# Spaced row scatters, quartered weight loads, later row norms and a written-out loop in an attention and expert kernel

## The reference, cut to what matters

```python
h = _layernorm(x) * (1 + ca) + sa
Q, K, V = heads(h, Wq), heads(h, Wk), heads(h, Wv)
scores = Q @ K.T / scale + lambda_attn * (tanh(Q) @ J_attn) @ tanh(K).T
scores = where(causal, -inf, scores)
x = x + ga * (softmax(scores) @ V @ Wo.T + bo)
h = _layernorm(x) * (1 + cb) + sb
expert = argmax(h @ centroids.T)              # one expert of 8 per token
alpha = sigmoid(h . centroids[expert])
y = h + relu(norm(h)*g[expert]+b[expert] @ W1[expert].T + b1[expert]) @ W2[expert].T + b2[expert]
x = x + gb * (alpha * y + (1 - alpha) * h)
```

## Time and profile before

| | |
|---|---|
| median of 3 runs | 809.66 us (809.44 to 812.22) |
| profiled execution | 811.99 us, of which its span is 810.2 us |
| instructions in the span | 17292 |
| mean granted clock of TensorE | 0.939 of full speed |
| TensorE matmuls, busy | 693.0 us (86%) |
| VectorE, busy | 545.7 us (67%) |
| ScalarE, busy | 503.0 us (62%) |
| GpSimd, busy | 259.3 us (32%) |
| DMA, mean | 114 GB/s |

### The profile page before, as it was taken

The page is one execution under the profiler, slowest core; times in us unless marked ns, Lnnn a source line. Parts: engine busy times, 40 slices in busy tenths (PEclk is TensorE's granted clock), DMA queues, the critical chain, the costliest instruction groups (busy, mean ns, idle before and its releaser), DMA issues.

```text
span 810.2 us, 17292 instructions
## 1 busy us (share of the span) xinstructions
PE 693.0 (86%) x5199; PEld 344.7 (43%) x5199; DVE 545.7 (67%) x1249; ACT 503.0 (62%) x1182; POOL 259.3 (32%) x342
## 2 busy tenths in 40 slices
PE   4467999999999999978999998799798889897594
PEld 2252434334334434423344343244343225886594
DVE  6959667787856777745568767478587611798352
ACT  1440677676688767745877676466576578657372
POOL 2028129000214724330156253200344100456543
PEclk9866799999999999978999999799899799999898
DMA  8995914193260708260516093526123353533510
GB/s 226 320 177 216 157 32 133 55 186 76 51 118 2 234 4 157 44 189 29 94 26 210 3 157 60 173 52 121 33 100 100 111 181 96 162 94 118 178 57 10
DMA packets 54723, 92.04 MB, mean 114 GB/s; under 512 B 10161, under 2 KB 26061, under 8 KB 54120
## 3 DMA queue, kind: packets, MB, share of 16 engines
q1 hardware_dynamic: 48444, 79.72, 39.4%
q0 software_dynamic: 3520, 8.42, 3.1%
q10 hardware_dynamic: 2668, 2.78, 1.2%
HBM read 51.04 MB, written 37.90 MB: 110 GB/s over the span
## 4 chain that ended last, share of the span: by engine, by line
PE 55%; DVE 18%; issue 10%; ACT 8%; DMA 4%; another core or an unknown queue 2%; POOL 1%; DVEq 1%; ACTq 1%; SPq 0%; POOLq 0%
PE PS L1248 14%; PE PS L1208 13%; PE PS L1274 13%; ACT arenaA L1030 5%; DVE PS L1694 4%; PE PS L1325 3%; PE PS L1336 3%; DVE block_max L1701 3%; PE PS L1278 2%; DVE arenaA L1371 2%; DVE arenaB L1371 2%; ACT arenaB L948 2%; PE PS L1213 2%; DMA arenaB<-r_den 1%
## 5 line engine op out<-in xcount | busy, mean ns | idle before, releaser
L1030 ACT ACTIVATE arenaA<-PS 128x512 f32<-128x512 f32 (+3 forms) x768 | 333.1, 495 | 188.3 <-PE PS L1278 127.3
L1694 DVE CUSTOM_DVE_ANT_0 PS<-PS,mask 128x1024 f32<-128x1024 f32 (+3 forms) x256 | 261.7, 1035 | 119.0 <-PE PS L1208 104.8
L1274 PE MATMUL PS<-arenaA 99*128 99x512 bf16 (+3 forms) x768 | 228.9, 342 | 30.7 <-ACT arenaA L1030 18.7
L1208 PE MATMUL PS<-arenaA 96*128 96x512 bf16 (+3 forms) x768 | 207.5, 347 | 30.3 <-DVE block_max L1701 10.0
L1274 PEld LDWEIGHTS PS<-arenaA 99*128 99x128 bf16 x768 | 73.2, 99 | 223.7 <-ACT arenaA L1030 143.7
L1248 PE MATMUL PS<-arenaA,Vs 128*9 128x512 f32 (+3 forms) x1536 | 161.1, 496 | 0.0
L1701 DVE TENSOR_REDUCE block_max<-PS 128x8 f32<-128x1024 f32 (+1 forms) x96 | 100.4, 1046 | 37.6 <-PE PS L1213 30.5
L1208 PEld LDWEIGHTS PS<-arenaA 96*128 96x128 bf16 x768 | 68.6, 102 | 99.9 <-DVE maxima L1694 30.5
L1278 PE MATMUL PS<-after,identb 128*128 128x128 bf16 x512 | 105.7, 224 | 0.0
L842 POOL DMA_INDIRECT out_dram<-arenaA x46 | 46.7, 1016 | 103.2 <-DVE arenaA L1371 94.8
L1079 ACT ACTIVATE arenaA<-PS,b1p 128x128 f32<-128x128 f32 x184 | 52.7, 373 | 34.5 <-PE PS L1325 20.1
(11 more groups left out here) (219 smaller groups left out, 687.8 us busy)
## 6 DMA issues: line engine op xcount, KB each, us to landing
arenaA<-k_parts SPq DMA_DIRECT2D x96, 128.0 KB, 8.2
arenaA<-by_expert SPq DMA_DIRECT2D x46, 192.5 KB, 3.7
o_raw<-OT SPq DMA_DIRECT2D x32, 256.0 KB, 3.3
k_parts<-arenaB SPq DMA_DIRECT2D x24, 256.0 KB, 3.8
arenaA<-q_parts SPq DMA_DIRECT2D x16, 384.0 KB, 4.9
q_parts<-arenaB SPq DMA_DIRECT2D x18, 256.0 KB, 3.7
arenaA<-in_L_ffn_W_dram SPq DMA_DIRECT2D x2, 2048.0 KB, 13.2
arenaA<-q_parts SPq DMA_DIRECT2D x16, 256.0 KB, 5.7
```

Of the source, the lines that this page charges most:

```text
L1030: a.activation(PT[:, u % EB, h, off:HALF], PS[:, 4 + n % SB_, off:HALF], ACT.Exp).then_inc(exp_ok, 1)
L1208: last = mm(PS[:, place + c0 // HALF, at:at + c1 - c0], SQ(g, h)[0:KROWS, t * P:(t + 1) * P], SK(g, h)[0:KROWS, c0:c1], start=(at == 0), s ...
L1274: last = mm(bank[:, off:HALF], SK(g, h)[0:MROWS, kb * P:(kb + 1) * P], SQ(g, h)[0:MROWS, qc * HALF + off:(qc + 1) * HALF], start=True, sto ...
L1694: v.tensor_tensor_reduce(out=src, in0=src, in1=mask[:, S - n:S], scale=1.0, scalar=-3e38, op0=ALU.add, op1=ALU.max, accum_out=maxima[:, pl ...
```

## The change

Four things are changed. (1) `scatter_rows` gets the number of a group, and block t of the eight waits until 2 + t units of products of that group are done. The group is the fourth of the body in which the rows are made (middle bodies), and the third of the last body. (2) The turned weights come back in four DMAs of 512 KB in place of one of 2 MB, the k-th of them k units of products later. (3) In the last body the norms of x move from units 0 and 1 of group 1 to units 2 and 3, and all items of `POST_LAST` in group 1 (H0, H1, statistics of h, S, the choice of the expert) one step later. (4) The loops over the middle bodies are Python loops, so that the code of each body stands in the program; the waits compare with constants, and the `sem_inc`s on the `..._turn` semaphores behind them are gone.

```diff
+        W_PARTS = 4
...
-        NORMS_AT = dict(middle=dict(x=(2, 0), h=(3, 0)), last=dict(x=(1, 0), h=(2, 0)))
+        NORMS_AT = dict(middle=dict(x=(2, 0), h=(3, 0)), last=dict(x=(1, 2), h=(2, 0)))
...
-                     1: POST_AT[2], 2: POST_AT[3] + ((9, "D", "pads"),), 3: ((0, "D", "table"),)}
+                     1: tuple((at + 1, kind, k) for at, kind, k in POST_AT[2]), 2: POST_AT[3] + ((9, "D", "pads"),), 3: ((0, "D", "table"),)}
...
                     if body == "last" and g < 2:
-
-                        sp.wait_ge(pv_ok, (b * NG + g + 1) * NU + EB)
-                        sp.dma_start((W1T, W2T)[g], w_turned[:, g * E * FF:(g + 1) * E * FF]).then_inc(w_back, 16)
+                        for k in range(W_PARTS):
+
+                            sp.wait_ge(pv_ok, (b * NG + g + 1) * NU + EB + k)
+                            part = slice(k * E * FF // W_PARTS, (k + 1) * E * FF // W_PARTS)
+                            sp.dma_start((W1T, W2T)[g][:, part], w_turned[:, g * E * FF:(g + 1) * E * FF][:, part]).then_inc(w_back, 16)
...
-            with sp.Fori(1, B - 1) as b:
+            for b in range(1, B - 1):
                 attention(b, "middle")
...
-            def scatter_rows(b):
+            def scatter_rows(b, group):
 
                 pool.wait_ge(pool_step, b * 4 + 4)
-                pool.sem_inc(pool_turn, 1)
                 pool.wait_ge(slots_ok, b + 1)
-                pool.sem_inc(pool_turn, 1)
                 pool.wait_ge(pay_ok, b + 1)
                 pool.sem_inc(rows_made, 1)
                 for t in range(TB):
+
+                    pool.wait_ge(pv_ok, group * NU + EB + 2 + t)
                     g.indirect_dma_start(by_expert, bass.IndirectOffsetOnAxis(ap=slot[:, t:t + 1], axis=0), PAY[:, t, :], None)\
                         .then_inc(sorted_out, 16)
...
-            with pool.Fori(2, B) as b:
+            for b in range(2, B):
                 split_batch(b)
-                send_rows(b - 2)
-            send_rows(B - 2)
+                send_rows(b - 2, (b - 1) * NG + 3)
+            send_rows(B - 2, (B - 1) * NG + 2)
...
-                act.wait_ge(w_back, 32)
+                act.wait_ge(w_back, 2 * W_PARTS * 16)
...
-            with pe.Fori(1, B - 1) as b:
+            for b in range(1, B - 1):
                 attention(b, "middle")
```

More of the change, by code:

```diff
@@ L445, in prepared @@
                 sp.wait_ge(va_ok, b + 1)
-                sp.sem_inc(sp_turn, 1)
             for n in (1, 2):
@@ L484, in load_numerators @@
             def load_numerators(b):
-                if isinstance(b, int):
+                if b >= B - 2:
                     sp.wait_ge(stored, B)
@@ L791, in send_rows @@
                 row_factors(b)
-                scatter_rows(b)
+                scatter_rows(b, group)
                 pool.wait_ge(sorted_out, (b + 1) * TB * 16)
@@ L874, in tanh_q @@
                 act.wait_ge(q32_ok, b + 1)
-                if not (isinstance(b, int) and b == 0):
+                if b > 0:
                     act.wait_ge(stored, b)
@@ L880, in first_q @@
             def first_q(b):
-                if not isinstance(b, int):
+                if b > 1:
                     act.wait_ge(sent, b - 1)
@@ L908, in norm_rows @@
                     act.wait_ge(stored, b)
-                    act.wait_ge(lnt_ok, 1 if isinstance(b, int) else 2)
-                    if not isinstance(b, int):
+                    act.wait_ge(lnt_ok, min(b, 2))
+                    if b > 1:
                         act.wait_ge(rows_made, b - 1)
-                        act.sem_inc(act_turn, 1)
                 row = lambda k: lnt[:, k, bass.ds(b * TB + t, 1)]
@@ L1067, in _ @@
             attention(0, "first")
-            with act.Fori(1, B - 1) as b:
+            for b in range(1, B - 1):
                 attention(b, "middle")
@@ L1139, in project @@
                 else:
-                    start = isinstance(b, int) and b == 0
+                    start = b == 0
                     if start and step == "K0":
@@ L1458, in projected @@
                 part = slice(half * HALF, (half + 1) * HALF)
-                later = not isinstance(b, int) or b > 0
+                later = b > 0
                 if what == "X":
@@ L1490, in after_routing @@
                 dve.wait_ge(route_chain, b * ROUTE_LINKS + n)
-                if not isinstance(b, int):
-                    dve.sem_inc(dve_turn, 1)
             L2 = lambda k: ln2[:, k, :]
@@ L1502, in half_stats @@
                 if half:
-                    last.then_inc(post_chain if isinstance(b, int) and b == B - 1 else done, 1)
+                    last.then_inc(post_chain if b == B - 1 else done, 1)
             def half_norm(b, dst, src, half):
@@ L1674, in maximum @@
                 if kind == "T":
-                    if not (isinstance(group, int) and group == 0):
+                    if group > 0:
                         dve.wait_ge(m_in, group * 16)
@@ L1781, in _ @@
             attention(0, "first")
-            with dve.Fori(1, B - 1) as b:
+            for b in range(1, B - 1):
                 attention(b, "middle")
```

25 lines of the change are left out of this document (4 added, 21 removed).

## The result

The changed kernel takes 774.36 us (median of 6 runs, 772.42 to 775.99), the kernel before in the same comparison 809.55 us: a ratio of 0.9554 [0.9528, 0.9579]. The profiled execution takes 773.26 us, its span is 771.5 us, and the two spans differ by 38.7 us. The kernel before was timed again beside each later set of runs, and its median there went up to 811.75 us; a difference between medians of two sets is good to about 2 us.

A forecast was written before the change was run, and what follows sets the result against it. TensorE bounds most of the span; gains lie in gaps at row-block bursts, the loop's jump and the norms. 811.99 - 14.5 - 5.2 - 5.3 - 1.4 = 785.6 us profiled; median 809.66 - 26.4 = 783.3 us, range 775 to 795.

The forecast's parts named there:

- Spacing: Groups with row blocks: one block per unit of products wins back 5.9 + 5.6 + 3.0 = 14.5 us of 19.0 excess.
- yardstick of 17.57 us: First body's group 3, no burst, unit 1's products to transposed maxima; the burst groups' excess over it: 7.4, 7.1, 4.5 us.
- residue of 1.5 us: Loss left in each burst's place after spacing, chosen between 0 and 8 x 2.49 us.
- Rival (a): Groups with bursts: all 19.0 us come back, 30.9 us in all, 778.8 us; chance 0.15.
- (b): Groups with bursts: stops belong to the traffic as a whole, spacing gives nothing; only 11.9 us, 797.8 us; chance 0.12.
- (e): Each of 24 spaced blocks stops the fetch by itself, 2.49 us a time; slower, 838.6 us; chance 0.03.
- Quarters: Turned weights in four pieces on SyncE: their waits cost nothing, and they get no term of their own.
- Norms: Last body, norms two units later: ScalarE no longer waits 4.01 us for moments; the whole 5.2 us excess counted.
- rival (c): Last body: the norms' move gives nothing, TensorE being held at the turn of those rows; 788.5 us; chance 0.10.
- Loop: Middle bodies written out: the jump goes, 5.3 us, and register work ahead of waits, 1.4 us.
- register work: Middle bodies, ahead of waits: 0.7 us a body, 1.4 in all; may be zero, 3 at most.
- Rival (d): Loop's end costs the same written out, pages of code coming late for another reason; 788.6 us; chance 0.05.

The follow-up runs named there:

- d1: Changed kernel with GpSimd's wait for units of products taken out, so the eight row blocks start back to back once the slots are known: 799.44 us, 0.9862.
- b5: Changed kernel with batch 3's batch statistics moved from group 3 of the first body to a late unit of its group 2: 773.41 us, 0.9553.
- a4: Kernel before with the spacing, the quarters and the norms' place, the two middle bodies still one loop with registers: 782.05 us, 0.9639.
- f1: Changed kernel, eight blocks back to back once slots are known, SyncE's ten transfers beside them in the middle bodies held back five units: 797.33 us, 0.9844.
- b1: Changed kernel with the eight row blocks back to back, but not before the ninth unit of products after the stacks: 796.29 us, 0.9816.
- f2: Changed kernel plus five back-to-back indirect blocks of 16 rows, 4 columns each, into an unread tensor; real blocks spaced, two units later: 792.16 us, 0.9772.
- d2: Changed kernel plus five back-to-back indirect blocks of 128 rows, 385 columns, into an unread tensor; real blocks spaced, two units later: 783.25 us, 0.9651.
- d4: Changed kernel plus five full blocks sent as plain transfers from GpSimd's queue to consecutive rows; real blocks spaced, two units later: 777.65 us, 0.9588.
- d3: Changed kernel plus five back-to-back indirect blocks of 128 rows, 4 of 385 columns, into an unread tensor; real blocks spaced, two units later: 783.06 us, 0.9646.
- e4: Changed kernel plus five back-to-back indirect blocks of 64 rows, 4 columns each, into an unread tensor; real blocks spaced, two units later: 786.69 us, 0.9711.
- b2: Changed kernel with two row blocks back to back for every two units of products: 775.71 us, 0.9577.
- e2: Changed kernel with the row blocks sent in two bursts of four, at units 2 and 6 of the group: 777.79 us, 0.9609.
- a2: Changed kernel with each group's turned weights read back in one transfer, as before the change: 774.40 us, 0.9547.
- a3: Changed kernel with the last body's row norms of x back at their old place, operations behind them not shifted: 777.83 us, 0.9585.

## Why the forecast was 9 us short, step by step

**Spacing: forecast 14.5 us, measured 25.1 by medians and 22.4 by the stretches (d1).** This step failed, by size and not by direction. The yardstick of 17.57 us held 1.8 us of statistics that the other groups lack (b5), 5.4 us in three bursts; and the residue of 1.5 us that I left in each burst's place, 4.5 us, did not appear: R1 is 15.83 where an empty group is 15.77. With both put right the term would have been 24.4; 2.0 of that belong to the loop, which makes R1, R2 and R3 longer by 0.49, 0.48 and 1.08 us with spaced blocks (a4), and 22.4 is what d1's three groups lose. Rival (a) erred by the yardstick too. Rivals (b) and (e) fell: the stop is gone with full traffic in place (in the changed kernel the DMA share of 346 to 354 is 1.03 to 1.10, and TensorE is busy throughout), and 24 single blocks stop nothing.

I had also read the chain of waits short: behind the 2.49 us of the earlier trace rows it stands a second time for the same burst, and the two make 6.9 us. The 2.49 went into the upper bound and into rival (e).

```profile
350.89 4.38 another core or an unknown queue
```

**What the stop is.** I took it for instructions that arrive late. That is not borne out: in the kernel before, no packet of the two instruction queues moves between 506 and 518, while the stop goes from 507.68 to 513.78 and ends. Only these two queues have packets in that window, and neither is an instruction queue (packets, MB, share of 16 engines):

```profile
q1 hardware_dynamic: 1034, 1.68, 52.6%
q0 software_dynamic: 512, 1.58, 38.9%
```

What the runs show is that ScalarE and VectorE get what TensorE has for them late while GpSimd issues indirect blocks one right behind the other. The semaphore events of the traces show it directly. In the changed kernel all 192 units of products raise `pv_ok` within 0.05 us of their recorded end. In the kernel before five do not, all beside a burst: the products that end at 507.23 raise it at 512.28, 5.05 us late, and the others are 0.98 to 3.21 us late. In d1 and f1 the latest is 5.6 us late, in b1 6.5, in f2 3.9, in d2 1.45; in d4 none beside the plain transfers is over 0.06. (The ends of matmuls are modelled, so the end of the work and the signal can't be told apart.) Bytes do not matter (d3), nor SyncE's transfers (f1), and fewer rows do not lessen it (e4, f2); plain transfers do not do it (d4), and pairs and fours cost little (b2, e2). Through what TensorE's signals are held, and why fewer rows make it worse, stays open; that the shorter distance of 1.15 us does it was not tested by itself.

**Quarters: forecast nothing, measured nothing (a2).**

**Norms: forecast 5.2 us, in place 6.4, but only 3.5 by themselves (a3).** ScalarE's 4.01 us wait was rightly read and is gone, and TensorE is not held at the turn of those rows: it turns them at 561.77 and idles 0.45 us behind, so rival (c) fell. Unforeseen was that writing out the loop takes 1.7 us from GpSimd's chain to the moments in the last body as well.

**Loop: forecast 5.3 + 1.4 us, measured 7.7 (a4).** The jump is 4.0 to 4.8 us and not 5.3, since I compared it with a first body whose stretch is not the same. The register work, 1.4 forecast, is 1.5 in the groups of the middle bodies and 0.55 at the entry; R3 and the stretch ahead of it, in the last body, are 1.1 and 0.3 us longer too; I had priced nothing there, since no register is read, and did not test whether the counts behind the waits make it. Rival (d) fell.

By medians the parts are 25.1 + 0.0 + 3.5 + 7.7 = 36.3 us, against 35.2 for all together; by ratios to the kernel before they are 24.9 - 0.6 + 2.5 + 6.9 = 33.7 against 36.1. Of the 8.8 us that the forecast lacked, the spacing alone has 10.6 by medians and 7.9 by the stretches; the norms' 1.7 us too much and the loop's 1.0 too little nearly cancel.

## What to carry to other kernels

Five or more indirect DMAs of GpSimd sent back to back held up the other engines here, for nearly as long as the row of them lasted and however small they were. Let each wait for a unit of TensorE's work, which costs nothing where nobody waits for the last. A stretch without the disputed thing is a yardstick only if it holds the same other work: list what stands in both before subtracting. And undo a part exactly as it was, for a burst 3 us later cost 9 us less.

## What the runs showed of the hardware

Eight indirect blocks of 128 rows at 1.27 us each stop ScalarE in the two middle bodies for 3.2 to 6.1 us at a stretch (3.19 and 6.10 us in before, 5.16 and 3.36 in d1, 5.86 and 4.69 in f1), and the whole group loses 6.4 to 8.5 us (d1 and f1). From unit 8 they stop it for 8.34 and 6.85 us (b1), and in the tail, with writes of tiles behind them, for 12.22 us. Meanwhile TensorE's `pv_ok` is raised up to 5.6 us late (d1, f1; 6.5 in b1); beside blocks 2.1 to 3.0 us apart it is never over 0.05 us late. Five indirect blocks of 16 rows, 4 columns each, lose 4.5 to 5.1 us a group (f2); five plain transfers of the same tensor's full rows lose 0.0 in the groups (d4). By the Trainium skill ("DMA: Bandwidth & Descriptors", section "Queues, rings and completion order") each DMA engine takes its queues in turn, packet by packet. The prediction's rival (b) drew from it that spacing gains nothing. The runs differ from that: spacing gains 22 to 25 us, and the stop comes with SyncE's transfers held back (f1) and at a DMA share of 0.43. The measurement decides; whether the engines keep to the rule itself no run here shows.

At the loop's jump two packets of an instruction queue move while TensorE stands idle (378.4 to 381.1 in the kernel before), where the stop of 507.68 to 513.78 has none.

A wait with a count on a second semaphore behind it takes 0.1 us more on GpSimd than the wait alone: 0.38 to 0.40 us a step in place of 0.28, in a chain of 22 steps.
